# First layernorm folded into a centred query weight, float32 projections of rows laid out by the host, the second norm on VectorE, and the branch one pair later

## What is computed

```
def _layernorm(x, axis=-1, eps=1e-05):
    m = jnp.mean(x, axis=axis, keepdims=True)
    v = jnp.var(x, axis=axis, keepdims=True)
    return (x - m) / jnp.sqrt(v + eps)
...
        q = x @ Wq.T
        k_raw = context @ Wk.T
        v_raw = context @ Wv.T
...
        q = _rmsnorm(q)
        k = _rmsnorm(k)
        scale = HEAD_DIM ** (-0.5)
        scores = jnp.einsum('bhnd,bhmd->bhnm', q, k) * scale
        attn = jax.nn.softmax(scores, axis=-1)
        out = jnp.einsum('bhnm,bhmd->bhnd', attn, v)
...
            W = (wq.astype(jnp.float32) - ZERO_POINT) * scale[:, None]
...
        gate = jax.nn.silu(gate)
        up = _qlinear(x, wq_up, s_up)
        return _qlinear(gate * up, wq_down, s_down)
    x = x + jnp.tanh(g_xattn[0]) * _L0_xattn_ref(_layernorm(x, axis=-1), ctx_2048, L0_xattn_Wq, L0_xattn_Wk, L0_xattn_Wv)
    x = x + jnp.tanh(g_ffn[0]) * _L0_ffn_ref(_layernorm(x, axis=-1), L0_ffn_wq_gate, L0_ffn_s_gate, L0_ffn_wq_up, L0_ffn_s_up, L0_ffn_wq_down, L0_ffn_s_down)
```

## Time and profile before

| | us |
|---|---|
| median of 3 runs | 254.41 (253.95 to 255.11) |
| profiled execution, its own time | 253.98 |
| its span | 252.2 |
| outside the span | 1.8 |
| PE busy | 211.7 (84%) |
| DVE busy | 186.6 (74%) |
| ACT busy | 176.5 (70%) |
| POOL busy | 107.4 (43%) |

### The profile page before, as it was taken

One profiled execution on the slowest core, in us unless ns is written; L12 is line 12 of the kernel. 1 busy time (PEld: TensorE's weight loads), 2 busy tenths in 40 slices (PEclk: granted clock), 3 DMA queues, 4 the chain that ended last, 5 costly groups with the idle time before them and its releaser, 6 DMA issues.

```text
span 252.2 us, 7331 instructions
## 1 busy us (share of the span) xinstructions
PE 211.7 (84%) x2592; PEld 173.7 (69%) x2592; DVE 186.6 (74%) x587; ACT 176.5 (70%) x338; POOL 107.4 (43%) x145
## 2 busy tenths in 40 slices
PE   1544796939878999999999999999999988983974
PEld 1434564727567888887888887888787876772973
DVE  5487999982677497969796968778697977668163
ACT  3349485735893889689878968896889689464260
POOL 5003303131133344465464728472846372554542
PEclk9995598985995999999999999999999999999799
DMA  6697360906061504060506051504324251000001
GB/s 183 184 352 211 77 90 0 108 6 104 3 61 46 106 2 86 23 146 0 104 0 146 0 104 22 123 13 95 71 56 41 45 77 55 21 25 0 21 21 42
DMA packets 45127, 18.08 MB, mean 72 GB/s; under 512 B 36400, under 2 KB 44848, under 8 KB 45104
## 3 DMA queue, kind: packets, MB, share of 16 engines
q1 hardware_dynamic: 45104, 17.77, 33.3%
HBM read 7.28 MB, written 2.10 MB: 37 GB/s over the span
## 4 chain that ended last, share of the span: by engine, by line
PE 62%; DVE 21%; issue 6%; ACT 5%; DMA 2%; POOL 2%; SPq 1%; DVEq 0%; ACTq 0%
PE bank L1375 16%; PE bank L1290 12%; PE pv_ps L1254 11%; PE bank L1399 8%; PE score_ps L1235 6%; PE bank L1323 3%; DMA w_raw<-L_xattn_Wv_dram 2%; DVE hidden L1002 2%; PE bank L1277 2%; DVE sums L908 2%; DVE x_stats L802 2%; ACT probs L531 1%; DVE silu L987 1%; PE bank L1281 1%; PE bank L1355 1%
## 5 line engine op out<-in xcount | busy, mean ns | idle before, releaser
L531 ACT ACTIVATE probs<-score_ps 128x1024 f32<-128x1024 f32 x64 | 66.0, 1033 | 2.8 <-PE score_ps L1235 2.7
L1375 PE MATMUL bank<-x_hi,gu_hi 128*128 128x256 f32 (+1 forms) x192 | 50.7, 300 | 4.4 <-DVE x_lo L1032 2.4
L467 POOL TENSOR_TENSOR qk_unit<-qk_raw,root_y 128x512 f32<-128x512 f32 x16 | 17.3, 1084 | 85.1 <-DVE root_y L792 85.1
L1254 PE MATMUL pv_ps<-probs,v_blocks 128*32 128x128 f32 x1024 | 43.4, 290 | 6.4 <-issue 3.9
L1375 PE MATMUL bank<-x_lo,gu_hi 128*128 128x256 f32 (+1 forms) x192 | 48.5, 285 | 0.0
L435 POOL TENSOR_TENSOR h_lo<-hidden,h_hi 128x256 fp32r<-128x256 f32 (+1 forms) x48 | 36.7, 772 | 20.6 <-ACT h_hi L657 19.5
L1375 PEld LDWEIGHTS bank<-x_hi,gu_hi 128*128 128x128 f32 (+1 forms) x192 | 35.4, 184 | 8.5 <-issue 5.0
L1254 PEld LDWEIGHTS pv_ps<-probs,v_blocks 128*32 128x32 f32 x1024 | 25.2, 113 | 16.1 <-issue 6.9
L1375 PEld LDWEIGHTS bank<-x_lo,gu_hi 128*128 128x128 f32 (+1 forms) x192 | 35.7, 186 | 0.0
L1290 PE MATMUL bank<-w_hi,xc_hi 128*128 128x256 f32 x96 | 30.3, 316 | 3.4 <-DVE xc_lo L898 3.3
L646 ACT ACTIVATE tanh_g<-bank,half_gate 128x256 f32<-128x256 f32 (+1 forms) x48 | 22.7, 473 | 13.1 <-PE bank L1375 11.4
(11 more groups left out here) (112 smaller groups left out, 434.0 us busy)
## 6 DMA issues: line engine op xcount, KB each, us to landing
ctx_sb<-ctx_dram SPq DMA_DIRECT2D x16, 128.0 KB, 2.4
out_dram<-x_all SPq DMA_DIRECT2D x16, 128.0 KB, 1.8
x_all<-x_dram SPq DMA_DIRECT2D x1, 1536.0 KB, 11.3
dn_int<-L_ffn_wq_down_dram SPq DMA_DIRECT2D x1, 704.0 KB, 7.6
gu_int<-L_ffn_wq_gate_dram SPq DMA_DIRECT2D x1, 640.0 KB, 4.6
gu_int<-L_ffn_wq_up_dram SPq DMA_DIRECT2D x1, 640.0 KB, 5.6
x_all<-x_dram SPq DMA_DIRECT2D x1, 384.0 KB, 5.3
w_raw<-L_xattn_Wq_dram SPq DMA_DIRECT2D x1, 256.0 KB, 3.0
```

What stands on the lines that cost most here:

```text
L531: nc.scalar.activation(probs[:, t % 2, :], score_ps[t % 2][:].rearrange("p h n -> p (h n)"), ACT.Exp, scale=float(HD) ** 0.5 / UNIT ** 2). ...
L1254: last = nc.tensor.matmul(pv_ps[BLOCK * quadrant:BLOCK * (quadrant + 1), region * P:(region + 1) * P], v_blocks[:, e, h * BLOCK:(h + 1) * ...
L1375: last = nc.tensor.matmul(bank[k][0:r, a * TOK:(a + 1) * TOK], w[:, j, a, c, 0:r], xx[:, c, :], start=(n == 1), stop=(n == (4 if wide_weig ...
```

## The change

Six things are changed together.

1. The host lays out the inputs: `turned` holds x and the context with the features on the partitions, `qkv` the three attention weights with features on partitions and heads in the kernel's order, and the integer weights are laid out likewise. PE no longer turns any of them: `turn`, the weight transposes and `prep` go, with their ScalarE and VectorE parts. The integer weights' upper parts are now converted directly by ScalarE in p = 0, the lower parts by GpSimd in p = 0 and 1, in pieces of two instructions (`lower_gate_up`, `lower_down`).
2. The projections are plain float32 matmuls, two for each of queries, keys and values (6 instead of 18 for a tile).
3. The first layernorm is not applied to x. Its mean is removed by subtracting from each column of the query weight that column's mean over the features (`average_queries` on PE, `centre_queries` on VectorE, once). Its scale cancels in the head norm, except in the epsilon, which becomes `epsilon[tile] = (variance + 1e-5) * 8e-6 / 4096` and is added to the sums of squares.
4. The second norm's row is written by VectorE in one instruction (`normalize2`), no longer by ScalarE.
5. The largest weight is found from squares summed by ScalarE in p = 1 (`square_weights`), and the branch on PE stands at the end of p = 1, ahead of the first two chunks, no longer at the end of p = 0.
6. The bank table loses the two `turn` tasks, and the DMAs of the context become DMAs of `turned` (256 KB for a tile instead of 128 KB).

```
-    BANK_OF = {"turn0": 0, "out0": 2, "v0": 1, "qk0": 0, "ffn2": 1, "ffn3": 2, "ffn4": 0, "ffn5": 1, "turn1": 2,
-               "out1": 0, "v1": 1, "qk1": 2, "turn2": 1, "y0": 2, "y1": 0, "ffn0": 2, "ffn1": 1}
+    BANK_OF = {"out0": 0, "v0": 1, "qk0": 2, "ffn2": 0, "ffn3": 1, "ffn4": 2, "ffn5": 0,
+               "out1": 1, "v1": 2, "qk1": 0, "turn2": 1, "y0": 2, "y1": 0, "ffn0": 1, "ffn1": 2}
...
+            sp.dma_start(xc[:, 0], turned[0]).then_inc(xc_loaded[0], 16)
+            for m in (1, 0, 2):
+                sp.dma_start(w[:, m], qkv[m]).then_inc(w_loaded[m], 16)
+            sp.dma_start(x_all[:, 0, :], x[0]).then_inc(x_loaded[0], 16)
...
+            def lower_gate_up(j):
+
+                source = gu_int[:, j] if j < NJ - 1 else gu_int_rest[:]
+                r = rows(j)
+                raw = whole[:, 0:2 * KC * r].rearrange("p (a c n) -> p a c n", a=2, c=KC)
+                pool.wait_ge(gu_hi_ready, j + 1)
+                nc.gpsimd.tensor_scalar(raw, source, ZERO_POINT, None, ALU.subtract).then_inc(whole_ready, 1)
+                pool.wait_ge(whole_ready, j + 1)
+                nc.gpsimd.tensor_tensor(gu_lo[:, j, :, :, 0:r], raw, gu_hi[:, j, :, :, 0:r].bitcast(F32),
+                                        ALU.subtract).then_inc(lo_ready, 1)
+                pool.wait_ge(lo_ready, j + 1)
...
                 split_qk(p, 0)
                 split_chunks(p, 2, (3, 4, 5))
+                if isinstance(p, int) and p in (0, 1):
+                    for j in range(3 * p, 3 * p + 3):
+                        lower_gate_up(j)
                 add_attention(p, 1)
                 qk_norm(p, 1)
                 split_qk(p, 1)
...
+                if isinstance(p, int) and p == 1:
+                    for i in range(4):
+                        lower_down(i)
...
+            def square_weights(i):
+
...
+                nc.scalar.activation(weight_squares[0:r, i % 2, 0:source.shape[1]], source, ACT.Square,
+                                     accum_out=weight_max[0:r, i:i + 1]).then_inc(w_squared, 1)
...
+            def centre_queries():
+
+                dve.wait_ge(w_averaged, 1)
+                for c in range(KC):
+                    last = nc.vector.tensor_tensor(wq_centred[:, c, :], w[:, 0, c, :], averages(), ALU.subtract)
+                last.then_inc(wq_ready, 1)
...
+                    nc.vector.scalar_tensor_tensor(out=root_in[:, 0:2 * H].rearrange("p (a h) -> p a h", a=2),
+                                                   in0=sums[:].rearrange("p (a h) -> p a h", a=2), scalar=UNIT ** -2,
+                                                   in1=epsilon_of(b + 2).to_broadcast([P, 2, H]),
+                                                   op0=ALU.mult, op1=ALU.add).then_inc(eps_added, 1)
...
+                nc.vector.tensor_scalar(x1n[:, 1 - e, :], tile_of(b), x1_mean_var[:, 0:1], root_y[:, 2 * H:],
+                                        ALU.subtract, ALU.mult).then_inc(x1n_ready, 1)
...
+            def project(dst, tile, source, weights):
+
+                for c in range(KC):
+                    last = nc.tensor.matmul(dst, xc[:, tile, source, c, :], weights[:, c, :], start=(c == 0), stop=(c == KC - 1))
+                return last
...
                 down(p, 1, wide_weights)
+                if not (isinstance(p, int) and p == 1):
+                    first_chunks(p, wide_weights)
...
             pe.wait_ge(rest_zeroed, 1)
-            pe.wait_ge(w_max_steps, 8)
+            pe.wait_ge(w_max_steps, 3)
             any_wide = pe.alloc_register("any_wide")
             pe.reg_load(any_wide, wide[:])
             with pe.If_ne(any_wide, 0):
-                run(pe, lambda p: iteration(p, True), 1)
+                first_chunks(1, True)
+                run(pe, lambda p: iteration(p, True), FIRST_STEADY)
             with pe.Else():
-                run(pe, lambda p: iteration(p, False), 1)
+                first_chunks(1, False)
+                run(pe, lambda p: iteration(p, False), FIRST_STEADY)
```

More of the change, by code:

```diff
@@ L706, in iteration, with early @@
             def iteration(p):
-                first = isinstance(p, int) and p == FIRST
+                def early(q, work, *args):
+                    if isinstance(p, int) and p == q:
+                        work(*args)
                 square(p, 0)
@@ L720, in iteration @@
                 upper(p, 2, 2)
-                if isinstance(p, int) and p == PAIRS - 1:
-                    normalize2(p, 0)
+                early(0, convert_gate_up, 1)
+                early(1, square_weights, 1)
                 tanh_chunk(p, 2, 4)
@@ L754, in iteration @@
                 drain_y(p, 0)
+                early(0, convert_gate_up, 4)
+                early(0, convert_gate_up, 5)
                 exp_octet(p, 1, 3)
-                if not (isinstance(p, int) and p == 0):
-                    normalize2(p, 1)
+                early(0, convert_down)
                 drain_y(p, 1)
@@ L992, in up @@
                 task = f"ffn{j}"
[L993 removed]
+                if not here(p, task):
                     return
@@ L1123, in iteration @@
                     roots(p, 0, 4, 7)
-                    x1_offset(p, 0)
+                    normalize2(p, 0)
                     gate(p, 2, 4)
                     up(p, 2, 4)
-                elif second:
-                    for n in range(1, ROOT_STEPS + 1):
-                        roots(p, 0, n, n)
-                        x_roots(2, n, n)
-                    x_offsets(2)
-                    gate(p, 2, 2)
-                    gate(p, 2, 3)
                 else:
```

544 lines of the change are left out of this document (189 added, 355 removed).

## The result

The changed kernel takes 263.65 us (262.08 to 263.76, four runs) against 254.18 (252.74 to 255.11, four runs): ratio 1.0363, 95% interval 1.03 to 1.0427, slower. The profiled execution took 263.58, its span is 261.8 us; before, 253.98 and 252.2. So 9.6 us of span are to be placed.

| PE at | before | after | difference |
|---|---|---|---|
| first scores | 27.04 | 23.20 | -3.84 |
| first matmul of chunk 0, p = 1 | 76.58 | 85.65 | +9.07 |
| first `weigh` of p = 2 / 3 | 80.26 / 105.11 | 89.33 / 114.61 | +9.07 / +9.50 |
| the same of p = 4 / 5 / 6 | 128.94 / 152.75 / 176.91 | 139.32 / 164.00 / 188.68 | +10.38 / +11.25 / +11.77 |
| the same of p = 7 / 8 | 200.80 / 222.09 | 212.70 / 233.66 | +11.90 / +11.57 |

The account below looks back on a forecast made before the run. PE was taken to bound the middle pairs, a loop of VectorE and GpSimd the start. Span 252.2 + 4.6 - 0.4 - 1.0 = 255.4, plus 1.8 around it: 257.2 us, range 250.5 to 262.

Parts of the forecast that it names:

- chunk 0: End of the start, p = 1: PE's chunk 0 begins at 81.2 instead of 76.58, 4.6 us later.
- the pairs up to p = 7: Saturated middle: float32 projections less the dropped transposes give -0.04 us a tile, -0.4 us over ten tiles.
- the last pair: End of the kernel: the last `turn2` starts earlier, VectorE's gates of chunks 4 and 5 0.3 later; -1.0 us.
- a piece is 1.9 us, bounds 1.7 and 2.4: GpSimd in p = 0 and 1: time of each two-instruction lower-weight piece, three of them behind the split in each pair.
- first scores: Start: PE's first scores at 25.0 instead of 27.04, between 23.2 and 25.2; two us gained.
- the dearer projection enters, no change: Start, p = 0: from first scores to first square stays 6.1 us, as turned rows leave and float32 projections enter.
- rival A: Start: the late branch and GpSimd's pieces eat what the start gains; 255.7 to 260.5 us, chance 0.50.
- PE drops four transposes for each tile, from 129.84 to 130.43: 0.59 us: Middle pairs: the removed transposes save PE 0.59 us a tile, against 0.55 more for the float32 projections.
- Hidden: Middle: ScalarE's and VectorE's changed work, `normalize2` included, lies beside a full PE; the 256 KB DMA has 12 us to land.
- C: PE's projections: float32 records cost no more than float32r ones, -1.3 us a tile, 244.5 us; chance 0.08.
- D: PE's projections: a float32 matmul costs 0.57 us, +0.7 a tile, 264.4 us; chance 0.10.
- start at about 231: Last pair: the last `turn2` starts there instead of 232.50, its bank and VectorE's row being ready earlier.

Follow-up runs that it names:

- run 1: Changed kernel without GpSimd's ten pieces (the lower halves of the feed-forward weights): 257.91 us, ratio 1.0135 to the kernel before.
- run 5: Changed kernel with the test of the largest weight (squares, reduction, DMA, comparison) moved earlier in p = 1: 259.06 us, ratio 1.0195 to the kernel before.
- run 6: Changed kernel with the early test and GpSimd's ten pieces behind a branch of GpSimd's own: 250.92 us, ratio 0.9837 to the kernel before.
- run 10: Changed kernel with early test, pieces behind GpSimd's branch, values projected before turned output rows, second norm on ScalarE in pairs 2 to 7: 248.58 us, ratio 0.9804.
- run 2: Changed kernel without TensorE's wait, load and branch on the largest weight and without the wide program; test kept: 258.04 us, ratio 1.0136 to the kernel before.
- run 4: Changed kernel with the values of each pair's first tile projected ahead of the turned output rows: 257.85 us, ratio 1.0173 to the kernel before.
- run 11: Changed kernel with early test, pieces behind GpSimd's branch, values projected before turned output rows, and half of each projection's contraction left out: 237.38 us, ratio 0.9337.
- Run 3: Changed kernel with the second layernorm's scaling back on ScalarE, with VectorE's small offset instruction: 266.07 us, ratio 1.0481 to the kernel before.
- run 8: Changed kernel with projections from the third pair on as three float32r products, halves made by ScalarE and VectorE: 275.15 us, ratio 1.0785 to the kernel before.

## Why the prediction missed

The direction was right (slower, which had 0.60); 263.65 lies outside the range of 250.5 to 262.0. By its own terms:

| term | predicted | measured |
|---|---|---|
| chunk 0 | +4.6 | +9.07 |
| the pairs up to p = 7 | -0.4 | +2.50 |
| the last pair | -1.0 | -1.97 |
| sum of span | +3.2 | +9.6 |

**The start: the step that failed is "a piece is 1.9 us, bounds 1.7 and 2.4".**

| step | predicted | measured |
|---|---|---|
| first scores | 25.0 (23.2 to 25.2) | 23.20 |
| split end, p = 0 | 37.6 | 37.29 |
| one piece | 1.9 | 2.94 |
| addition of p = 0, e = 1 | 43.3 | 46.05 |
| addition of p = 1, e = 0 | 53.9 | 56.51 |
| split end, p = 1 | 61.0 | 64.04 |
| addition of p = 1, e = 1 | 66.1 | 71.60 |
| `x_lo` end | 70.3 | 75.90 |
| comparison end | 77.1 | 81.00 |
| chunk 0 | 81.2 | 85.65 |

Three pieces of 2.94 for 1.9 are 3.1 us in p = 0; in p = 1, 7.5 for 5.1 are 2.4. That is the 5.5 us of the addition in p = 1. My lower neighbour for the first instruction was a memset, which reads nothing, and my upper one the split. It takes 1.49 us, over both: the bound was no bound, since neither row reads int32. That the type is the reason is likely but not shown, as no run has this instruction with a float32 source. The second takes 1.27, as against 1.16. The Trainium skill ("GPSIMD Engine Reference", 4.1 Engine selection) calls elementwise work on GpSimd some two times slower than on VectorE with two inputs, and "roughly line-rate" with one. The rows don't bear out that one input is the cheaper case here: 1.49 us for the one-input instruction with an int32 source, 1.27 for the two-input one in float32. The pieces' weight is 5.7 us alone (run 1), and 8.1 when the test is early (run 5 to run 6).

The other steps of the start nearly cancel. The first scores came at my lower bound, 1.8 us early: the first transpose was issued at 18.31, and didn't wait for the end of the load. In other runs with the same start they came at 22.82 (run 10) to 24.66 (run 6), so that this step is less sure than the one trace says. But "the dearer projection enters, no change" was wrong: from the first scores to the first square went 7.4 us, not 6.1. The block of projections took 4.6 us there (25.94 to 30.57, granted clock 0.62 from 25 to 31), where the 18 matmuls before took 2.9. The row of maxima was in SBUF 2.0 us after its reduction, not 3.5; before, its DMA was issued at 47.83, 0.8 us behind a load of context rows, and after, nothing had been issued for more than 10 us; no run tests whether that is the reason. From the comparison to chunk 0 went 4.65 us, not 4.1. And two errors cancel in the steps at 50.57 and 76.59: the norm took 1.26 us for my 0.4, and `qk_parts` behind it 0.68 for my 1.5, since it is the norm that now runs beside GpSimd's scaling. That is luck, not a right price.

That the late branch eats the start's gain, rival A's mechanism, was right: without it chunk 0 follows `x_lo` (run 2). The branch and the pieces hide each other: with the pieces away 5.7 us are won, with the early test 4.6 (run 5), with both 12.7 (run 6).

**The middle: the step that failed is "PE drops four transposes for each tile, from 129.84 to 130.43: 0.59 us".** PE's work came out as written: 2.8 us a block, and 23.58 a pair. But at e = 0 the transposes had stood in front of a group that waits for ScalarE's exponential. They were cover, not cost: 2.37 us before and after. Between the groups of `weigh` one can read the rest: at e = 1 the stretch with the turned rows fell from 3.23 to 2.79 us, the stretch with the projections of e = 0 grew from 3.15 to 3.69, that with the projections of e = 1 and `turn2` from 3.66 to 4.59, and the others lost 0.15. That makes +0.88 a pair, where I had -0.08. Run 4 settles it: with other work in the gap, 23.85.

The price at `turn2` comes from the sentence under "Hidden" that VectorE's work lies beside a full PE. Rows of the changed kernel: VectorE's `qk_parts` beside GpSimd's scaling, the norm beside it, and the norm alone:

```profile
34.36 0.69 DVE L855 TENSOR_TENSOR qk_parts<-qk_raw,root_y 128x512 f16<-128x512 f32 x1
34.41 1.58 POOL L451 TENSOR_TENSOR qk_unit<-qk_raw,root_y 128x512 f32<-128x512 f32 x1 [9.20 <-DVE root_y L742]
...
50.57 1.26 DVE L827 TENSOR_SCALAR x1n<-x_all,x_mean_var,root_y 128x256 f32<-128x256 f32 x1
50.61 1.07 POOL L451 TENSOR_TENSOR qk_unit<-qk_raw,root_y 128x512 f32<-128x512 f32 x1 [3.83 <-DVE root_y L742]
...
62.62 0.40 DVE L827 TENSOR_SCALAR x1n<-x_all,x_mean_var,root_y 128x256 f32<-128x256 f32 x1
```

The instruction takes 0.40 alone, and 1.26 when GpSimd's scaling starts with it. I took 0.4 and named 1.2 as the bound; in the middle it is 0.82 at e = 0 and 1.28 at e = 1, so the bound was the value. The Trainium skill ("SBUF — State Buffer", SBUF: two separate sides) says that the port pair of the two engines is an exclusive lock, whose loser waits for the whole instruction. The rows agree that one of the two waits: at 34.41 GpSimd's scaling takes 1.58 instead of 1.07 and VectorE keeps its 0.69, at 50.57 it is VectorE. They don't agree in full: there VectorE's start is recorded 0.04 us ahead of GpSimd's, and its 1.26 is 0.2 less than both durations in turn (1.07 and 0.40). Run 3 gives the share of it: 0.36 us a pair. Run 10 gives none once the gap is filled.

**Float32.** 0.45 us a matmul was right, 2.8 a block in the middle, so rivals C and D are out. Its other effect I had missed. "The dearer projection enters, no change" is wrong for the start: a block there takes up to 5.1 us (run 1), and run 11 gives 2.0 to 3.55 us for half of it. The Trainium skill ("FP8 and Floating Point Precision", TensorE Precision Notes) has four passes for true FP32, 2.96 a block by the float32r row; at the full clock the block took 2.8, so the rule is nearly met.

**The last pair.** The step "start at about 231" was worth 1.0; it gave 0.4. From the first `weigh` of p = 8 to `turn2` went 10.41 us before and 10.03 after: the bank's wait is gone, but the row that VectorE writes is late too (2.44 us of wait for `x1n`). The rest I had not seen. Rows of the kernel before and of the changed one:

```profile
240.99 0.39 PE L1375 MATMUL bank<-x_hi,gu_hi 128*128 128x256 f32 x1 [1.54 <-DVE hidden L1002]
```

```profile
243.69 0.63 PE L1185 MATMUL bank<-ident,x1n 128*128 128x128 f32 x4 [2.44 <-DVE x1n L827]
```

Chunk 2 of p = 9 had the bank of chunk 1 and waited 1.54 us for its gate. In the new table it has another bank, and this wait is gone.

The number expected of run 11 was right by two errors that cancelled, a middle that gave 2 us and not 8, and a start that gave 2.0 to 3.55 which I had not counted. Such a hit is no support.

**Left open.** Whether it is the int32 source that makes the first instruction of a piece 1.49 us. What float32r halves made in a better place would give (run 8 put them in a bad one). Which waits make up VectorE's chain of 23.5 us a pair; run 11 shows that it is there, not what shortens it.

## What to carry to other kernels

When an instruction is taken from the engine that is never idle, ask what the next one in its queue waits for. If that is set by another engine, the instruction was cover and its time comes back as a wait; put other work in its place and look again.

Work for a program that rarely runs should stand behind the test that chooses it. Here ten pairs of GpSimd instructions for the wide weights stood between an attention output and its addition, and a test that nobody needed until then stood behind everything else; moving both, with the order of run 4, turned 3.6% slower into 3.3% faster.

A bound from the nearest rows is safe only if they read the same data type and have the same engine at work beside them.
